# A message stage written out step by step with three load slots, and a different split of the row scatters between two stages of a graph network kernel

## The reference

```python
h = relu(layernorm(x))
x = x + gat(h)               # attention over incoming edges and a self loop, per node
h = relu(layernorm(x))
x = x + cfconv(h)            # message passing with a filter from the edge attributes

def gat(h):                  # 4 heads of 32
    m = leaky_relu((h @ W_l)[s] + (h @ W_r)[d], 0.2)
    e = einsum('ehc,hc->eh', m, att)
    e = exp(e - segment_max(e, d)[d]); alpha = e / segment_sum(e, d)[d]
    return segment_sum(alpha[:, :, None] * (h @ W_l)[s], d) + bias

def cfconv(h):               # ssp(x) = softplus(x) - log 2
    w = (ssp(edge_attr @ Wf1 + bf1) @ Wf2 + bf2) * edge_weight[:, None]
    agg = segment_sum((h @ W_in2f)[dst] * w, src)
    return ssp(agg @ Wo1 + bo1) @ Wo2 + bo2
```

## Time and profile before

| what | value |
|---|---|
| median of 3 runs | 3317.54 us (3313.77 to 3329.19) |
| the profiled execution's own time | 3332.83 us |
| its span, first to last instruction | 3331.0 us |
| mean granted TensorE clock | 0.908 of full speed |
| attention stage, start of the first and last store of a_xo's rows | 653.8 to 1793.0 us |
| message stage, start of the first and last b_y | 1800.5 to 2897.9 us |
| GB/s moved by the DMA engines, by 1/40 of the span, in both edge stages | 102 to 130 |

### The profile page before, as it was taken

The page is one execution under the profiler, slowest core; times in us unless marked ns, Lnnn a source line. Parts: engine busy times, 40 slices in busy tenths (PEclk is TensorE's granted clock), DMA queues, the critical chain, the costliest instruction groups (busy, mean ns, idle before and its releaser), DMA issues. The chain is left out here.

```text
span 3331.0 us, 58371 instructions
## 1 busy us (share of the span) xinstructions
PE 2544.2 (76%) x16674; PEld 1760.3 (53%) x16674; DVE 2454.0 (74%) x6275; ACT 2194.7 (66%) x4803; POOL 1916.5 (58%) x1633
## 2 busy tenths in 40 slices
PE   6776777788887877787886777777777777758887
PEld 5554555444443444444444665666555565547776
DVE  7554555678887877887787778777878778737776
ACT  6655666667777777777775555555555555549998
POOL 2564555267766666766752777777777777720000
PEclk9877899989999999999998889788899899979999
DMA  7665566333333333333333666666666666679998
GB/s 239 241 229 187 212 215 214 118 117 130 127 126 116 130 116 129 118 128 116 124 102 102 117 116 116 115 113 117 119 117 119 116 117 118 114 261 404 424 422 350
DMA packets 323596, 558.99 MB, mean 168 GB/s; under 512 B 135552, under 2 KB 211828, under 8 KB 285794
## 3 DMA queue, kind: packets, MB, share of 16 engines
q1 hardware_dynamic: 226290, 448.50, 40.1%
q0 software_dynamic: 97200, 109.30, 16.6%
HBM read 324.12 MB, written 242.20 MB: 170 GB/s over the span
## 5 line engine op out<-in xcount | busy, mean ns | idle before, releaser
L665 POOL DMA_INDIRECT sum_dram<-b_sum,b_at x392 | 641.1, 1636 | 233.3 <-issue 117.2
L589 POOL DMA_INDIRECT a_xd<-in_x,index x344 | 361.5, 1051 | 162.4 <-issue 100.0
L580 POOL DMA_INDIRECT a_xs<-in_x,index x344 | 364.5, 1060 | 146.8 <-issue 101.6
L598 POOL DMA_INDIRECT x_dram<-a_xo,index x196 | 211.4, 1079 | 290.7 <-DVE a_xo L900 191.7
L1330 PE MATMUL bank<-wl,turned 128*128 128x128 f32 x1568 | 263.8, 319 | 74.4 <-ACT turned L1106 54.4
L802 DVE TENSOR_TENSOR d_x<-bank,d_x 128x512 f32<-128x512 f32 x196 | 134.7, 687 | 239.0 <-remote 142.6
L1330 PEld LDWEIGHTS bank<-wl,turned 128*128 128x128 f32 x1568 | 222.5, 219 | 134.4 <-ACT turned L1106 89.5
L1109 ACT ACTIVATE d_n<-d_x,stat_d_shift,stat_d_rstd 128x128 f32<-128x128 f32 x686 | 283.3, 485 | 0.2 <-DVE stat_d_shift L701 0.2
L1453 PE MATMUL bank<-b_rows,b_same 128*128 128x128 bf16 x4704 | 279.9, 219 | 0.6 <-ACT b_sum L1246 0.6
L1486 PE MATMUL bank<-wo,f_ssp_out 128*128 128x128 f32 x1568 | 225.3, 287 | 55.9 <-DVE f_ssp_out L1055 51.9
L1453 PEld LDWEIGHTS bank<-b_rows,b_same 128*128 128x128 bf16 x4704 | 265.1, 98 | 0.6 <-issue 0.6
(11 more groups left out here) (191 smaller groups left out, 7025.7 us busy)
## 6 DMA issues: line engine op xcount, KB each, us to landing
d_x<-in_x SPq DMA_DIRECT2D x49, 1024.0 KB
x_dram<-d_x SPq DMA_DIRECT2D x49, 1024.0 KB
out<-d_x SPq DMA_DIRECT2D x49, 1024.0 KB, 7.6
sum_dram<-zero SPq DMA_DIRECT2D x48, 1024.0 KB
d_x<-x_dram SPq DMA_DIRECT2D x45, 1024.0 KB, 12.0
d_n<-sum_dram SPq DMA_DIRECT2D x25, 1024.0 KB, 9.1
x_end_dram<-a_xo SPq DMA_DIRECT2D x98, 256.0 KB
b_x<-x_end_dram SPq DMA_DIRECT2D x98, 256.0 KB
```

The costliest lines, as they stand in the source:

```text
L580: pool.indirect_dma_start(a_xs[t % DEPTH][:, j * F:(j + 1) * F], None, x, column(t, j)).then_inc(gathered[t % GSEM], 16)
L589: pool.indirect_dma_start(a_xd[t % DEPTH][:, j * F:(j + 1) * F], None, x, column(t, TILES + j)).then_inc(gathered[t % GSEM], 16)
L598: pool.indirect_dma_start(x1_dram, column(t, 2 * TILES + j), a_xo[t % 4][:, j * F:(j + 1) * F], None, bounds_check=bound, oob_is_err=False ...
L665: pool.indirect_dma_start(sum_dram, bass.IndirectOffsetOnAxis(ap=b_at[s][:, j:j + 1], axis=0), b_sum[s][:, j * F:(j + 1) * F], None, compu ...
```

## The change

- The message stage of all five engines is written out, step by step, in place of the loops. Addresses are constants.
- b_x, b_fa, b_goes, b_w and b_src have three buffers each (DB = 3) in place of two. The copies b_end, sidx and b_col are gone: VectorE and GpSimd read the tables in place.
- SyncE loads a step with one function, load_b(t). It waits until four uses of step t-3 are done (b_y, the transpose of b_fa, b_msg, b_same) and until its scatters have landed, and then issues all five loads. All five count on one semaphore, b_ld[t % 3], and every reader waits for all five.
- EARLY = (2, 1) in place of (2, 2): of every odd chunk, the attention stage scatters one row tile and the message stage three. That moves 49 scatters of 128 rows from the attention stage to the message stage.
- 12 in place of 8 of the a_xd buffers come before the place of the final stage's early loads, since the message stage's buffers need more room. No instruction changes by that.

```diff
-EARLY = (2, 2)
+EARLY = (2, 1)
...
+DB = 3
...
-            b_x = at2("b_x", [P, TILES * F])
...
+            b_x = [at(f"b_x{i}", [P, TILES * F]) for i in range(DB)]
...
-        a_xd = [sb(f"a_xd{i}", [P, TILES * F]) for i in range(DEPTH - 4 * (PRE - RX))]
+        a_xd = [sb(f"a_xd{i}", [P, TILES * F]) for i in range(DEPTH // 2)]
...
+        b_ld = sems("b_ld", DB)
+        x1_scattered = sems("x1_scattered", DB); added = sems("added")
...
+        def loaded(t):
+
+            return 16 * 5 * (t // DB + 1)
+
+        def scattered(t):
+
+            return 16 * sum(TILES - EARLY[1 - u % 2] for u in range(t % DB, t + 1, DB))
...
-            def load_rows_b(k, u, t0):
...
+            def load_b(t):
+
+                s = t % DB
+                if t >= DB:
+                    for sent in (b_y_ready, b_fa_turned, b_msg_ready, b_same_ready):
+                        sp.wait_ge(sent, t - DB + 1)
+                        sp.sem_inc(sync_step, 1)
+                    sp.wait_ge(x1_scattered[s], scattered(t - DB))
...
+                c = NC - 1 - t
+                sp.dma_start(b_x[s][:, :], x1_end_dram[c:c + 1, :, :].rearrange("o p f -> (o p) f")).then_inc(b_ld[s], 16)
...
+                sp.dma_start(b_goes[s][:, :], goes_dram[c:c + 1, :].broadcast_to([P, C])).then_inc(b_ld[s], 16)
+                sp.dma_start(b_w[s][:, :], weight_dram[c:c + 1, :].broadcast_to([P, C])).then_inc(b_ld[s], 16)
+                sp.dma_start(b_src[s][:, :], src_dram[c:c + 1, :].broadcast_to([P, C])).then_inc(b_ld[s], 16)
+
+            for t in range(NC):
+                load_b(t)
...
             def scatters(k, u):
-                s = u % 2
-                pool.wait_ge(sidx_ld[s], 16 * turn(k, u))
-                pool.wait_ge(b_x_ld[s], 32 * turn(k, u))
+                t = 2 * k + u
+                pool.wait_ge(b_ld[t % DB], loaded(t))
                 pool.sem_inc(pool_step, 1)
-                for j in range(EARLY[1 - s], TILES):
...
+                for j in range(EARLY[1 - t % 2], TILES):
+                    pool.indirect_dma_start(x1_dram, column(NC - 1 - t, 2 * TILES + j),
+                                            b_x[t % DB][:, j * F:(j + 1) * F], None,
+                                            bounds_check=bound, oob_is_err=False).then_inc(x1_scattered[t % DB], 16)
...
             def sums_b(k, u, t0):
                 s = u % 2
-                dve.wait_ge(b_x_ld[s], 32 * turn(k, u))
+                t = 2 * k + u
+                dve.wait_ge(b_ld[t % DB], loaded(t))
...
-            for u in range(4):
-                step_b(0, u, u, mid=u >= 1, back=u >= 2)
-            with dve.Fori(2, HALF - 1) as k:
-                for u in range(2):
-                    step_b(k, u, 4 + u)
...
+            for t in range(NC + 2):
+                step_b(t // 2, t % 2, t, ahead=t + 1 < NC, front=t < NC, mid=1 <= t <= NC, back=t >= 2)
```

More of the change, by code:

```diff
@@ L202, in at2 @@
                 return [at(f"{name}{i}", shape, dt) for i in range(2)]
-            b_x = at2("b_x", [P, TILES * F])
[L205 to L208, removed]
+            b_x = [at(f"b_x{i}", [P, TILES * F]) for i in range(DB)]
+            b_fa = [at(f"b_fa{i}", [P, TILES * 32]) for i in range(DB)]
+            b_goes = [at(f"b_goes{i}", [P, C], BF16) for i in range(DB)]
+            b_w = [at(f"b_w{i}", [P, C]) for i in range(DB)]
+            b_src = [at(f"b_src{i}", [P, C]) for i in range(DB)]
             b_y = at2("b_y", [P, TILES * F])
@@ L440, in step_b @@
[L440 to L455, removed]
@@ L470, in load_sums @@
+            for t in range(NC):
+                load_b(t)
+            for t in range(NC - DB, NC):
+                sp.wait_ge(x1_scattered[t % DB], scattered(t))
             def load_sums(g, slot):
@@ L666, in adds @@
                                             b_sum[s][:, j * F:(j + 1) * F], None, compute_op=ALU.add).then_inc(added[s], 16)
[L668 to L675, removed]
+            for t in range(NC):
+                scatters(t // 2, t % 2)
+                if t >= 2:
+                    adds(t // 2, t % 2 - 2, first=t == 2)
             for u in range(2):
@@ L948, in _ @@
                 dve.wait_ge(early_scattered[s], 16 * EARLY[s] * HALF)
-            for i in range(2):
+            for i in range(DB):
                 padded = b_fa[i][:, :].rearrange("p (j r) -> p j r", j=TILES)
@@ L972, in mask_b @@
                 dve.wait_ge(b_rstd, t + 1)
-                dve.tensor_tensor(st["sq"][:, 0:TILES], st["rstd"][:, 0:TILES], b_end[s][:, :], ALU.mult).then_inc(b_masked, 1)
+                dve.tensor_tensor(st["sq"][:, 0:TILES], st["rstd"][:, 0:TILES], ends[:, TILES * (NC - 1 - t):TILES * (NC - t)], ALU.mult).then_inc(b_masked, 1)
                 dve.wait_ge(b_masked, t + 1)
@@ L1022, in step_b @@
                     for j in range(TILES):
-                        last = dve.tensor_scalar(b_same[o][:, j, :], b_src[o][:, :], b_col[o][:, j:j + 1], None, ALU.is_equal)
+                        last = dve.tensor_scalar(b_same[o][:, j, :], b_src[c][:, :], columns[:, 8 * (NC - t) + j:8 * (NC - t) + j + 1], None, ALU.is_equal)
                     last.then_inc(b_same_ready, 1)
@@ L1464, in _ @@
             pe.wait_ge(load_weight, 16 * (2 + 2 * TILES))
[L1465 to L1471, removed]
+            for t in range(NC + 2):
+                step_b(t // 2, t % 2, t, front=t < NC, mid=1 <= t <= NC, back=t >= 2)
             def f_turn(c, q, slot, m, c0):
```

60 lines of the change are left out of this document (9 added, 51 removed).

## The result

The changed kernel takes 3483.28 us (median of 4 runs, 3480.94 to 3483.93), the kernel before in the same comparison 3323.36 us (4 runs): the change makes it **slower, ratio 1.048** (95% interval 1.045 to 1.051). The forecast was 3567 us in a range of 3430 to 3690.

A forecast was written before the change was run, and what follows sets the result against it. Waits between engines set the pace; after the change a ring of loads was to set 13.9 us a message step. 3332.8 + 246 + 3 = 3582, less 15.3 for the median, gave 3567 us, range 3430 to 3690.

The forecast's parts named there:

- The load's ring: Message stage: b_same releases five loads, b_y waits for all, one after the other each step; 13.9 us, ends 12.5 and 15.6.
- b_y to the end of b_same, 5.95 us: VectorE's part of the message step, from b_y's start to the end of b_same: mean of 6.19 and 5.71 us.
- rival (c): Message stage: slower by little, loads overlap more or VectorE's part shrinks; 11.7 to 12.4 us a step, +35 to +105; chance 0.08.
- b_x 2.85 us: Message stage, b_x's issue to b_y: 3.35 us, less 0.5 credited because the load of b_end falls away.
- the four other loads 4.9 us: Message stage: b_w, b_src, b_goes and b_fa, 696 thousand bytes at 141 GB/s, which b_y now waits for too.
- +246 us for the stage: Message stage: 95 steps growing from 11.31 to 13.9 us; ends +113 and +408.
- The scatters cost the message stage nothing: Message stage: half a scatter more a step, 0.69 us of GpSimd's work, costs nothing while the loads' ring is longer.
- GpSimd's 11.2 us as the next bound: Message stage: GpSimd's adds and scatters with issue gaps grow from 10.5 to 11.2 us a step, the next longest ring.
- The attention stage gives back 0: Attention stage: 68 us less scatter work only makes GpSimd wait longer for a_xo; 0, at most a few us back.
- 0 for fetching more code: Written-out message loops: fetching more code taken as 0, since engines have slack; at most 0.4 us a step.
- Rival (a): Message stage: loads fast enough, extra four under 2.2 us, GpSimd becomes the bound; 3307 to 3330 us, no change; chance 0.08.
- Rival (b): Attention stage: GpSimd holds it with late gathers, so fewer scatters bring it forward 68 us, to 3250 us; chance 0.04.

The follow-up runs named there:

- experiment 3: Changed kernel with b_x on a semaphore of its own, which b_y and the scatters wait for; against the kernel before, ratio 1.0006, message step 11.16 us.
- experiment 4: Changed kernel, one semaphore kept, with the wait on b_same moved down to the load of b_src; against the kernel before, ratio 1.0025, step 11.18 us.
- Experiment 5: Changed kernel without the 256 KB load of b_w after the first three steps; message step 11.68 us (one run) against the changed kernel's 13.24.
- experiment 1: Changed kernel with EARLY = (2, 2) again, the rest of the change kept; against the kernel before, ratio 1.068, message step 13.24 us.
- the first comparison: The changed kernel against the kernel before, as in the result: 3483.28 us against 3323.36 us, ratio 1.048.
- experiment 2: Kernel before with EARLY = (2, 1) and nothing else; against the kernel before, ratio 1.0039, message step 11.40 us in place of 11.12.
- the two kernels: Kernel before and changed kernel, both unchanged, in a comparison at 3000 us: 2998.8 us (one run) and 3199.7 us, ratio 1.066.
- The last kernel: Changed kernel with EARLY = (2, 2), b_x's own semaphore and the wait on b_same only ahead of b_src; 3270.27 us against the kernel before's 3315.9, ratio 0.986.
- experiment 6: Changed kernel with b_x's own semaphore and EARLY (2, 2), (3, 2), (3, 3): ratios 0.992, 1.012, 1.032; late b_same wait added: (3, 3) 1.008, (2, 2) 0.986.

## Why the prediction was right, and where its sizes were off

- *The load's ring decides, the third slot buys no lead.* Right: VectorE waits 391.5 us for the last load, which b_same releases, and experiments 3 and 4 open the ring at either end and take the message step from 13.24 to 11.16 and 11.18 us.
- *b_y to the end of b_same, 5.95 us, and 0.2 to the issue.* 5.71 and 0.17 in the mean of 95 steps. The 5.95 was read rightly, for before the change the same part is 5.92 us in the mean; it became shorter, as rival (c) had considered. That is 0.24 of the 0.51 us by which the ring was too long.
- *b_x 2.85 us and the four other loads 4.9 us.* Together 7.75, and measured 7.51 in the mean: 0.24 too long. b_x's part is confirmed by experiment 3, where b_y waits for b_x alone: 2.88 us from issue to b_y in the 23 steps that wait. That leaves 4.6 us for the other four, which is about 150 GB/s for their 696 thousand bytes, near the 141 that was taken; the 200 of the stretch with little else in it would have been too fast. Experiment 5 confirms that this term goes by bytes.
- *+246 us for the stage.* +188.0. The ring's mean of 13.39 in place of 13.9 us is 48 of the 58 us. Another 9 are a fault of the sum: the 11.31 us that were taken off for each of the 95 steps are the mean of all 97, and the two ahead of them took 14.1 us together before the change (b_y at 1800.49 and at 1814.63), so the others took 11.40. The last one is that those two took 13.3 us after it.
- *The scatters cost the message stage nothing.* Right while the ring is longer: experiment 1. And GpSimd's 11.2 us as the next bound is what experiment 3 ran into, with 11.16 us a step. GpSimd's waits, which were to grow by 2 us a step or more, grew by 1 (from 1.1 to 2.1): the half scatter more a step and the longer adds took the rest.
- *The attention stage gives back 0.* Wrong. I had argued from GpSimd's waits for VectorE's a_xo that GpSimd's load there does not matter. Those waits did grow, from 191.7 to 216.3 us, and the stage became shorter all the same. It is -40.6 us in the first comparison and -9.4 to -12 at 3000 us (experiments 1, 2 and the two kernels). The last kernel, with both edits and (2, 2), takes 1143.5 us there in a comparison like the first, like the kernel before, so it goes with the scatters. Through what they act was not isolated.
- *+3 us for the first b_y*: +2.8. *0 for fetching more code*: with the written-out code and the ring open, the kernel of experiment 3 runs as fast as the kernel before. More code is indeed fetched (the queues named "instruction" moved 1.43 MB in the message stage, and 0.08 MB before), but no cost of it shows in the total; one that the slack hides is not excluded.
- *VectorE's wait before b_y, 4.8 us a step and 450 us in all*: 4.2 and 391.5. *The step near 14 us*: 13.39.
- Rival (a), the loads being fast enough, needed less than 2.2 us for the extra loads; they took 4.6. Rival (b) had a part of its gain in it, 40.6 of 68 us, but not its sign; that gathers are late does not show, since in neither profile VectorE waits for a gather in that stage.

The two misses point the same way, 58 us too much in the message stage and 41 in the attention stage. Less the 15 us that I had taken off for the median (the changed kernel's profiled execution took as long as its median) they are the distance of 84 us from 3567 to 3483.

## What to carry to other kernels

A further buffer slot gives lead only if the release comes earlier with it: look up which use of a slot comes last in the step, and let only the load of that buffer wait for it. Loads that share a semaphore are as late as the last of them, so the first consumer should wait for its own alone. Either repair was enough here to be as fast as the old kernel; both together, with the scatters split (2, 2) as before, beat it by 1.4%. Price the loads that a step waits for by their bytes, at a rate measured beside the other traffic of the stage: 141 GB/s gave 4.9 us where 4.6 were measured, and the 200 GB/s of a stretch with little else in it would have given 3.5. And take the terms of a ring from many steps, without the first ones: single steps here lie between 12.3 and 15.0 us, and a mean that held two short steps gave 11.31 for 11.40.

## What the runs showed of the hardware that was not expected

- The kernel before takes 3323 and 3316 us in two comparisons and 3000 to 3004 us in the others, and the number of the chip does not tell them apart. The larger part of the difference lies ahead of the attention stage: the first a_xo starts at 646.6 us in the one profile and at 475.9 in the other. From first to last a_xo it is 1145.6 against 1003.3 us, and behind the last a_xo the two agree within 22 us. In the slower ones the attention stage has pauses of up to 6 us, before the change in about every fourth step, in which VectorE and ScalarE wait for something that the profile cannot name. Before the change and after it, in the first comparison, VectorE's were:

```profile
DVE a_run L886 <- remote: 38.4, 13, 4.7
DVE a_xo L900 <- remote: 26.6, 11, 3.7
```
```profile
DVE a_run L859 <- remote: 21.6, 6, 5.9
...
DVE a_run L856 <- remote: 10.9, 5, 2.4
...
DVE a_xo L870 <- remote: 6.9, 4, 1.8
```

  65.0 us in 24 pauses, and 39.4 in 15. 26 of the 40.6 us that the attention stage gained stand in these rows. The last kernel of experiment 6, with (2, 2), has 82.6 us in 28. At 3000 us there are none. What they are, and why fewer scatters go with fewer of them, stays open.
- The message step hardly differs between the two groups: 11.31 and 11.12 us before, 13.25 and 13.24 after.
- GpSimd's adds take 1763 ns in the mean in the changed kernel, 1636 before and 1642 in experiment 3, at the same shape. They run then, by the timelines, beside the burst of loads; that this is the reason was not tested.
